# Cross-attention with an FFN: attention scores as plain fp32 products on row halves, two heads at once

## The reference, cut to what matters

```python
q_big = jnp.einsum('bshk,hkq->bshq', q_hk, w_kc_q)
q_r = jnp.einsum('bshq,hqr->bhsr', q_big, W_qr)
k_r = jnp.einsum('bld,hdr->bhlr', kv_rope, W_kr)
scores = jnp.einsum('bhsr,bhlr->bhsl', q_r, k_r)
attn = jax.nn.softmax(scores, axis=-1)
ctx_c = jnp.einsum('bhsl,bld->bhsd', attn, kv_rope)
ctx_lat = jnp.einsum('bhsd,hkd->bshk', ctx_c, w_kc_kv)
out = ctx_lat.reshape(b, s, H * K) @ Wo.T
```

## Time and profile before

| | us | share of the span |
|---|---|---|
| median of three runs | 171.54 | |
| span of the profiled execution | 169.3 | |
| PE busy | 157.8 | 93% |
| DVE busy | 114.2 | 67% |
| ACT busy | 102.6 | 61% |
| POOL busy | 58.1 | 34% |

### The profile page before, as it was taken

How to read it: one execution, slowest core, us unless ns; L and a number is a source line. 1 busy time by engine, 2 the same in 40 slices (tenths; PEclk the granted TensorE clock), 3 DMA queues, 4 the chain that set the end, 5 groups by cost and what they waited for, 6 DMA issues and landing times.

```text
span 169.3 us, 3798 instructions
## 1 busy us (share of the span) xinstructions
PE 157.8 (93%) x1013; PEld 112.2 (66%) x1013; DVE 114.2 (67%) x297; ACT 102.6 (61%) x246; POOL 58.1 (34%) x89
## 2 busy tenths in 40 slices
PE   7486989999999999999999999999999999999863
PEld 7353648575866676666667575857586868877652
DVE  1485886785787477666858585778566939954782
ACT  3133569684858477947876685868496885523310
POOL 6317134232333234323433342423243221530460
PEclk9957999999999999999999999999999999999999
DMA  4953233533243223321332232231940000000002
GB/s 102 298 93 76 62 57 52 120 60 62 75 70 53 51 55 60 54 85 30 62 60 65 44 62 49 62 55 24 300 197 0 0 4 0 0 0 0 4 31 95
DMA packets 42696, 11.13 MB, mean 66 GB/s; under 512 B 39040, under 2 KB 41984, under 8 KB 42688
## 3 DMA queue, kind: packets, MB, share of 16 engines
q1 hardware_dynamic: 41632, 9.95, 27.0%
q0 software_dynamic: 256, 0.75, 1.3%
q10 hardware_dynamic: 800, 0.33, 0.8%
HBM read 10.50 MB, written 0.52 MB: 65 GB/s over the span
## 4 chain that ended last, share of the span: by engine, by line
PE 62%; DVE 15%; issue 8%; ACT 6%; DMA 3%; SPq 2%; POOL 2%; POOLq 0%; DVEq 0%; ACTq 0%
PE ctxb L778 16%; PE trans L767 11%; PE work L749 9%; PE score L759 7%; PE score L760 6%; ACT probs L417 4%; PE work L738 3%; DMA wq<-in_L_xattn_Wq_dram 3%; DVE q_hl L548 3%; PE work L728 3%; DVE w_ffn L594 3%; DVE neg_max L554 2%; ACT q_hl L412 2%; PE work L848 2%; PE work L734 2%
## 5 line engine op out<-in xcount | busy, mean ns | idle before, releaser
L359 POOL TENSOR_SCALAR probs<-probs,row_inv 128x512 f32<-128x512 f32 x64 | 45.4, 710 | 90.6 <-DVE row_inv L559 90.6
L417 ACT ACTIVATE probs<-score,neg_max 128x512 f32<-128x512 f32 x64 | 44.1, 689 | 34.8 <-DVE neg_max L554 34.6
L554 DVE TENSOR_REDUCE neg_max<-score 128x1 f32<-128x512 f32 x64 | 43.9, 686 | 14.8 <-PE score L760 13.3
L767 PE MATMUL trans<-ident,probs 128*128 128x128 f32 x256 | 39.4, 277 | 0.0
L423 ACT ACTIVATE probs_t<-trans 128x512 f32<-128x512 f32 x64 | 36.9, 591 | 3.7 <-PE trans L767 3.7
L767 PEld LDWEIGHTS trans<-ident,probs 128*128 128x128 f32 x256 | 30.0, 140 | 11.3 <-issue 4.1
L759 PE MATMUL score<-k_hi,q_hl 128*128 128x512 f32 x62 | 31.1, 502 | 0.3 <-ACT probs L417 0.2
L778 PE MATMUL ctxb<-probs_t,kv 128*64 128x256 f32 x240 | 29.2, 385 | 0.0
L760 PE MATMUL score<-k_lo,q_hl 128*128 128x512 f32 x62 | 24.5, 395 | 0.0
L778 PEld LDWEIGHTS ctxb<-probs_t,kv 128*64 128x64 f32 x240 | 15.9, 136 | 9.1 <-issue 1.5
L548 DVE TENSOR_TENSOR q_hl<-work,q_hl 64x256 fp32r<-64x256 f32 x32 | 13.5, 423 | 7.8 <-ACT q_hl L412 7.3
(11 more groups left out here) (108 smaller groups left out, 139.7 us busy)
## 6 DMA issues: line engine op xcount, KB each, us to landing
wq<-in_L_xattn_Wq_dram SPq DMA_DIRECT2D x8, 256.0 KB, 2.8
wo<-in_L_xattn_Wo_dram SPq DMA_DIRECT2D x64, 32.0 KB, 1.9
wk_wkr<-in_L_xattn_w_kc_q_dram SPq DMA_DIRECT2D x23, 64.0 KB, 2.4
pw<-in_L_ffn_pweight_dram SPq DMA_DIRECT2D x1, 1024.0 KB, 5.0
nw<-in_L_ffn_nweight_dram SPq DMA_DIRECT2D x1, 1024.0 KB, 7.0
wqr<-in_L_xattn_W_qr_dram SPq DMA_DIRECT2D x7, 96.0 KB, 2.0
wkv<-in_L_xattn_w_kc_kv_dram SPq DMA_DIRECT2D x8, 64.0 KB, 2.0
out_dram<-y SPq DMA_DIRECT2D x4, 128.0 KB, 1.7
```

The lines of the kernel that those rows point to most:

```text
L359: pool.tensor_scalar(e, e, row_inv[:, j:j + 1], 1.0, ALU.mult, ALU.mult).then_inc(norm_made, 1)
L417: act.activation(probs[:, j, :], score_bank[j % 2][:], ACT.Exp, bias=neg_max[:, j:j + 1], accum_out=row_sum[:, j:j + 1]).then_inc(exp_made, 1)
L554: dve.tensor_reduce(neg_max[:, j:j + 1], score_bank[j % 2][:], axis=AX, op=ALU.max, negate=True).then_inc(max_made, 1)
L767: last = pe.transpose(trans_bank[j % 2][:, lt * P:lt * P + P], probs[:, j, lt * P:lt * P + P], ident[:])
```

## The change

The high and low parts go. Keys are copied out once per batch by ACT into `k_t` (both copies, rows 0 to 63 and 64 to 127), and queries of both heads at once by DVE into `q_t` (head 0 in rows 0 to 63, head 1 in rows 64 to 127). Only even slots make scores: four plain fp32 products of 64 rows by 256 key columns, half by half and head by head, head h into `score_bank[h]`. Such a group waits until the exponential of tile t - 1 is made, so that both banks are free. Maxima, exponentials and all else keep their slots.

```diff
-            def k_high(b):
+            def take_keys(b):
                 act.wait_ge(k_transposed, b + 1)
-                act.activation(k_hi[:, b, :], trans_bank[b][:], ACT.Copy).then_inc(k_hi_made, 1)
-
-            def q_high(count, b, g):
-
-                act.wait_ge(work_made, count)
-                for h in range(2):
-                    act.activation(q_hl[0:64, 2 * b + h, :], g[64 * h:64 * h + 64, 0:S], ACT.Copy)\
-                       .then_inc(q_hi_made, 1)
+                act.activation(k_t[:, b, :], trans_bank[b][:], ACT.Copy).then_inc(k_taken, 1)
...
-            def k_low(b):
-                dve.wait_ge(k_hi_made, b + 1)
-                dve.tensor_tensor(k_lo[:, b, :], trans_bank[b][:], k_hi[:, b, :].bitcast(f32),
-                                  ALU.subtract).then_inc(k_taken, 1)
...
-            def q_low(p, b, g):
-
-                for h in range(2):
-                    dve.wait_ge(q_hi_made, 4 * p + 2 * b + h + 1)
-                    last = dve.tensor_tensor(q_hl[64:128, 2 * b + h, :], g[64 * h:64 * h + 64, 0:S],
-                                             q_hl[0:64, 2 * b + h, :].bitcast(f32), ALU.subtract)
-                last.then_inc(work_taken, 1)
+            def take_queries(p, b, n):
+
+                dve.wait_ge(work_made, q_count(p, b))
+                dve.tensor_copy(q_t[:, b, :], work[BANK_OF[n]][:, 0:S]).then_inc(work_taken, 1)
...
-            def scores(i, t, j):
-                b, h, tt = tile_of(j)
+            def scores(i, t, j, first=False):
+
+                b, _, tt = tile_of(j)
                 if j % (2 * TT) == 0:
                     pe.wait_ge(work_taken, q_count(i, b))
-                pe.wait_ge(exp_made, t - 1)
-                q = q_hl[:, 2 * b + h, tt * P:tt * P + P]
-                pe.matmul(score_bank[j % 2][:], q, k_hi[:, b, :], start=True, stop=False)
-                pe.matmul(score_bank[j % 2][:], q, k_lo[:, b, :], start=False, stop=True).then_inc(scored, 1)
+                if not first:
+                    pe.wait_ge(exp_made, t)
+                for half in range(2):
+                    for h in range(2):
+                        rows = slice(64 * h, 64 * h + 64)
+                        product = pe.matmul(score_bank[h][:, half * S:half * S + S], q_t[rows, b, tt * P:tt * P + P],
+                                            k_t[rows, b, half * S:half * S + S], start=True, stop=True)
+                        if half == 1:
+                            product.then_inc(scored, 1)
...
-                    if first and j < 2:
-                        scores_first(j)
-                    else:
-                        scores(i, t, j)
+                    if j % 2 == 0:
+                        scores(i, t, j, first=first and j == 0)
```

More of the change, by code:

```diff
@@ L59, in xattn_ffn_kernel @@
     f32 = mybir.dt.float32
-    f32r = mybir.dt.float32r
     ACT = mybir.ActivationFunctionType
@@ L127, in xattn_ffn_kernel @@
         kv = sb("kv", [P, B * LT, 2 * DC])
-        k_hi = sb("k_hi", [P, B, L], f32r)
-        k_lo = sb("k_lo", [P, B, L], f32r)
+        k_t = sb("k_t", [P, B, L])
         wk_wkr_t = sb("wk_wkr_t", [P, 4 * K + P])
@@ L138, in xattn_ffn_kernel @@
         m = sb("m", [P, DT, 2 * DC])
-        q_hl = sb("q_hl", [P, 2 * B, S], f32r)
+        q_t = sb("q_t", [P, B, S])
         n_all = sb("n_all", [P, NP, D])
@@ L191, in xattn_ffn_kernel @@
         k_transposed = sem("k_transposed")
-        k_hi_made = sem("k_hi_made")
         k_taken = sem("k_taken")
@@ L195, in xattn_ffn_kernel @@
         work_taken = sem("work_taken")
-        q_hi_made = sem("q_hi_made")
         scored = sem("scored")
@@ L431, in one_pair @@
                     if first and j == 2:
-                        k_high(1)
-                    if j == SLOT_OF[Q1]:
-                        q_high(q_count(i, 1), 1, work[BANK_OF[Q1]])
+                        take_keys(1)
                     hurried = j in (LAG - 1, LAG + 3)
@@ L442, in one_pair @@
                         exponentials(TILES * i + j, j)
-                    if j == SLOT_OF[Q0] and not last:
-                        q_high(q_count(i + 1, 0), 0, work[BANK_OF[Q0]])
                     if last and j == 0:
@@ L462, in _ @@
             take_step(M_)
-            k_high(0)
-            q_high(q_count(0, 0), 0, work[BANK_OF[Q0]])
+            take_keys(0)
             one_pair(0, first=True)
@@ L535, in _ @@
             first_stats(1)
-            k_low(0)
             def take_step(i, n):
@@ L617, in one_pair @@
                     if j == SLOT_OF[Q1] + 1:
-                        q_low(i, 1, work[BANK_OF[Q1]])
+                        take_queries(i, 1, Q1)
                     if not last:
@@ L625, in one_pair @@
                         if j == SLOT_OF[Q0]:
-                            q_low(i + 1, 0, work[BANK_OF[Q0]])
-                    if first and j == 2:
-                        k_low(1)
+                            take_queries(i + 1, 0, Q0)
                     if j == LAG and not first:
@@ L634, in one_pair @@
                         ffn_weights(j)
-            q_low(0, 0, work[BANK_OF[Q0]])
+            take_queries(0, 0, Q0)
             for t in range(TT, T):
@@ L834, in last_contexts @@
                 last.then_inc(ctx_made, 1)
[L836 to L843, removed]
             def project(t, p):
```

## The result

The changed kernel takes 188.39 us (median of four runs, 187.21 to 189.48) against 171.35 us for the kernel before on the same chip (four runs): a ratio of 1.098, 95% interval 1.094 to 1.102. The profiled execution's span is 186.7 us, 17.4 more than the 169.3 of before; it is the run of 188.94 us, 0.55 above the median. The ratios further down are to the kernel before as it was timed beside each experiment (medians of 171.08 to 172.09). One of the four runs of e1_pair_wait_alone and one of e10_both_first_e_later were longer at a lower clock; their medians count it and their ratios do not.

A forecast was written before the change was run, and what follows sets the result against it. PE, 93% busy, bounds the kernel; after the change the longer of PE's work and the DVE/ACT chain counts per block. Start -0.95, first round +1.2, loop +10.3, last +2.6: +13.2 on span 169.3, 182.5, timed 184.7 us; range 179 to 198.

The forecast's parts named there:

- S: Score products for two tiles on PE: eight paired row-half instructions, 1.02 us; 1.88 if one after the other.
- Rival 1: Row halves do not overlap, score group grows by 0.86 us, time about 205 us; chance 0.12.
- Rival 3: Halves overlap, but weights or mode changes cost 0.2 to 0.4 us more per score group: 191 to 198; chance 0.08.
- PE's own sum: PE's score work in a loop round: from 4.7 to 4.3 us, falling by only 0.4.
- A: Loop round, score group of slot 0 to slot 2: DVE and ACT chain 4.42 us against PE's work 3.24.
- C: Loop round, score group of slot 4 to slot 6: led by ACT's order, 3.90 us against PE's work 2.6.
- Rival 2: Chain stays covered in A and C, PE's work decides, kernel gets faster: 165.8 us; chance 0.07.
- B: Loop round, score group of slot 2 to slot 4: PE's work decides, 4.8 us; chain 4.3 to 4.4.
- D: Loop round, score group of slot 6 to next round's slot 0: PE decides, about 4.7 us; chain 4.35.
- Start: Before the first score product: one DVE query copy replaces ACT's and DVE's, start at about 15.35, -0.95 us.
- First round: Round ahead of the loop rounds: blocks of 3.9, 4.0, 3.9 and 4.7, 16.5 us against 15.27, +1.2.
- Last round: Round after the loop rounds: A 5.44 (+2.0), C about 6.8 (+0.7), B gives 0.1 back: +2.6 us.

The follow-up runs named there:

- e1_pair_wait_alone: Kernel before with its float32r products and copies, but two tiles scored together in even slots, waiting for the exponential of the tile just before: 199.51 us, ratio 1.164.
- e10_both_first_e_later: Kernel of e5_both_first with the preparation step at L734 moved behind the context products in the loop rounds: 181.36 us, ratio 1.054.
- single head: Changed kernel's fp32 arithmetic and copies, but one head per slot on one row half, with the old wait: 207.74 us, ratio 1.214.
- e5_both_first: Changed kernel with DVE's two maxima of a pair first, and ACT's two exponentials ahead of both transposed tiles in slots 0/1 and 4/5: 180.98 us, ratio 1.055.
- e3_transpose_later: Changed kernel with DVE's big weight transpose behind maximum 1 instead of between the two maxima, in the six loop rounds: 185.44 us, ratio 1.081.

## Why the prediction was right

The forecast was 184.7 us in 179 to 198; measured were 188.4. By its own steps:

- *Row halves overlap like column halves, S = 1.02.* Right; S is 1.07 (68.79 to 69.86), and the single head's 1.06 shows the overlap directly. Rival 1 is out. Rival 3 put its price on the score group, which came out only 0.05 over; dearer mode changes there are nevertheless, as the next step shows. The Trainium skill's ratio of 3.07 for four row tiles ("TensorE: Matmul & The Clock Gate", Part 3: Packing small matmuls), from which I had estimated 1.28 for S, does not carry over to these two halves.
- *PE's own sum falls by only 0.4 us a round.* Wrong, and without harm to the forecast, since the chain leads A and C. Busy time in a round rose from 15.98 to 16.49. Counted from start to start with the waits taken off, PE's own work in a round is about 16.1 us after and 15.7 before (my estimate from the two lists): 0.4 more instead of 0.4 less. The score groups do save 0.5 by the same count. But the prediction took what stands between them over from the old list, where a float32r product on the whole array follows the transposes after 0.36 us (66.85 to 67.21 in the earlier trace rows). Ahead of a group on row halves the same four transposes take 0.53. The list of e5_both_first shows it where nothing is waited for:

```profile
70.38 0.60 PE L750 MATMUL trans<-ident,probs 128*128 128x128 f32 x4
70.91 1.13 PE L740 MATMUL score<-k_t,q_t 64*128 64x256 f32 x8
```

  So PE's own work in A is 3.54 where the prediction had 3.24, and PE stood for 0.9 us there and not for 1.18. A shorter chain meets PE's own work sooner than I thought, in A at 3.54.
- *Block A 4.42, C 3.90, led by the chain.* Measured 4.44 and 3.88. The release by ACT's exponential stands at both. Rival 2 named the point from which it would decide, a turn-round under 3.24 in A and 2.6 in C; it was 4.4 and 3.9.
- *Blocks B 4.8 and D 4.7, led by PE.* Right in kind, 4.96 and 4.83. The miss, 0.29 a round and 1.7 us over six, is the term S (0.05 in each block) and about 0.1 in B and in D. In D I put that tenth down to the dearer mode changes of the step above. In B it is in part ACT: tile 7's copy ends at 76.18, and the context products behind it start at 76.31 instead of some 0.1 earlier.
- *Start, -0.95.* The first group starts at 15.46, forecast 15.35.
- *First round, 16.5.* 17.12 (15.46 to 32.58), 0.6 more.
- *Last round, +2.6.* This is the term that was mis-sized most. From S(0) to the end it took 45.5 us against 41.0, +4.4. Block A (5.50, forecast 5.44) and C (6.70, forecast 6.8) were right; B took 9.05 where 7.2 was forecast. About 1.6 of that is the fall of the clock (B takes 7.42 in the profiles without it), which I had not thought of; by their mean clocks two of the four runs were without it. The other 0.2 I have not taken apart.

So of the 17.4 us of span, 12.0 are the six loop rounds, 1.9 the first round, 4.4 the last, and 0.85 came back at the start, and the forecast of 13.2 missed 4.2 of them: 1.7 in the loop, 0.6 in the first round, 1.8 in the last, 0.1 at the start.

Another sentence of the prediction was right only in part, also without hurting the sum: that none of the copies is on PE's path in the loop. It held for the kernel before and for the kernel after, but only because the change removed them. With the pair wait and the old copies (e1_pair_wait_alone) the time is 11 us above the changed kernel's, and the lists show the copies in the chain. So the change is two things that had to come together: a schedule that costs 28 us, and an arithmetic with fewer copies that gives 11 of them back.

## What to carry to other kernels

When a change makes one operation wait for the release of all the buffers that it fills, write down for each stretch between two such waits both lengths, the waiting engine's own work and the chain through the others in their program order; the round is the sum of the longer ones, and busy shares say nothing about it. Everything queued between the two links of the chain (here a weight transpose, a copy, a transposed tile) becomes part of it, and moving it out helps only until the next consumer of that engine waits instead. Before packing two products side by side, price what they replace and the mode changes around them: two tiles at once cost as much here as two float32r tiles one after the other, so there was nothing to pay for the lost buffer with.

## What the runs showed of the hardware

- Two fp32 products of 64 rows on the two row halves of the array cost what one does: 1.07 us for eight instructions, 1.06 for four. The program's order of the two heads does not matter (1.07 either way).
- Four transposes take 0.36 us to the next start when a product on the whole array follows (66.85 to 67.21 before the change), and 0.53 when a group on row halves follows (70.38 to 70.91 in e5_both_first).
- The granted clock was at its lower level for 3.41 us in the last round of the changed kernel, just behind a wait of PE of 1.90 us, and stayed at 1.00 in e3_transpose_later behind the same wait; the fall cost 1.7 us.
